# Polynomial attention: state formed straight from scaled keys in 32x32 tiles, values of the four groups in different rows, outputs added up and projected once

## What is computed

```python
qkv = x @ W_attn
q, k, v = jnp.split(qkv, 3, axis=-1)       # 16 heads of 8 columns
...
att = jnp.einsum('bhid,bhjd->bhij', q, k) * (1.0 / math.sqrt(hd))
causal = jnp.tril(jnp.ones((T, T), dtype=bool))
att = jnp.where(causal[None, None], att, -jnp.inf)
att = polymax(att)      # s > 0: (s*s + 1)/1000; -100 <= s <= 0: (1 - 0.01*s)/1000; else 0
y = jnp.einsum('bhij,bhjd->bhid', att, v)
...
return y @ W_proj
```

## Time and profile before

| | |
|---|---|
| time, median of 3 runs | 3188.33 us (3187.82 to 3189.63) |
| the profiled execution's own time | 3197.16 us |
| its span, first to last instruction | 3195.4 us |
| mean granted TensorE clock | 0.919 of full |
| attention stage touched here | about 667 to 1341 us of the span |
| length of its steps | about 34 us; about 44 for the third group of an element in the loop; 48 with `finish` |

### The profile page before, as it was taken

The page is one execution under the profiler, slowest core; times in us unless marked ns, Lnnn a source line. Parts: engine busy times, 40 slices in busy tenths (PEclk is TensorE's granted clock), DMA queues, the critical chain, the costliest instruction groups (busy, mean ns, idle before and its releaser), DMA issues. The chain is left out here.

```text
span 3195.4 us, 55424 instructions
## 1 busy us (share of the span) xinstructions
PE 2832.2 (89%) x15400; PEld 1924.1 (60%) x15400; DVE 2087.3 (65%) x5242; ACT 1199.9 (38%) x2164; POOL 836.7 (26%) x1220
## 2 busy tenths in 40 slices
PE   5999999958787888689999998869989989999986
PEld 4777777735555555467777776445465465465453
DVE  6777777747676777577777776355556556555533
ACT  2111111127565657521111111335545545545532
POOL 1222332225555555423222332001101101111100
PEclk8999999958888788899999998879999999999988
DMA  3000000000000000110000000000000000000000
GB/s 130 0 0 0 0 0 0 1 0 2 3 2 3 2 2 2 61 44 0 0 0 0 0 0 1 0 1 1 1 2 1 1 1 1 1 1 1 1 1 27
DMA packets 12996, 23.60 MB, mean 7 GB/s; under 512 B 2306, under 2 KB 7682, under 8 KB 12804
## 3 DMA queue, kind: packets, MB, share of 16 engines
q1 hardware_dynamic: 12804, 21.22, 2.0%
HBM read 18.52 MB, written 2.10 MB: 6 GB/s over the span
## 5 line engine op out<-in xcount | busy, mean ns | idle before, releaser
L555 DVE SCALAR_TENSOR_TENSOR moe_acc<-moe_ps,moe_comb,moe_acc 128x512 f32<-128x512 f32 x896 | 661.1, 744 | 174.5 <-PE moe_ps L304 167.9
L2017 DVE CUSTOM_DVE_ANT_0 attn_masked<-attn_psm,attn_causal 128x1024 f32<-128x1024 f32 (+7 forms) x512 | 367.6, 755 | 210.4 <-PE attn_psm L1742 199.3
L1921 ACT ACTIVATE attn_probs<-attn_pse 128x512 f32<-128x512 f32 (+1 forms) x640 | 319.9, 553 | 301.6 <-PE attn_pse L1756 301.0
L304 PE MATMUL moe_ps<-moe_Wg,moe_xh 128*128 128x512 f32 x1024 | 329.4, 403 | 25.0 <-DVE moe_Wu L501 25.0
L335 PE MATMUL moe_ps<-moe_Wd,moe_ih 128*128 128x512 f32 x1024 | 337.8, 411 | 0.0
L304 PE MATMUL moe_ps<-moe_Wu,moe_xh 128*128 128x512 f32 x1024 | 337.1, 411 | 0.0
L1772 PE MATMUL attn_psy<-attn_probs,attn_V 128*64 128x512 f32 (+3 forms) x1536 | 325.5, 524 | 0.3 <-POOL attn_probs L1677 0.3
L454 POOL TENSOR_SCALAR moe_part<-consts,moe_pick,moe_prob 128x8 f32<-128x8 f32 x256 | 98.1, 398 | 752.1 <-ACT moe_prob L389 752.1
L1677 POOL TENSOR_SCALAR_AFFINE_SELECT attn_probs<-attn_probs 128x256 f32<-128x256 f32 (+1 forms) x192 | 95.1, 495 | 757.7 <-ACT attn_probs L1921 757.7
L1021 POOL TENSOR_TENSOR attn_R<-attn_R 128x1024 f32<-128x1024 f32 (+1 forms) x128 | 215.5, 1690 | 201.6 <-DVE attn_R L1365 201.4
L1756 PE MATMUL attn_pse<-attn_qS,attn_kS 110*128 110x512 f32 (+3 forms) x768 | 233.2, 394 | 21.4 <-ACT attn_probs L1921 15.2
(11 more groups left out here) (208 smaller groups left out, 4871.2 us busy)
## 6 DMA issues: line engine op xcount, KB each, us to landing
moe_stageg<-in_w_gate SPq DMA_DIRECT2D x8, 512.0 KB, 7.2
moe_stageu<-in_w_up SPq DMA_DIRECT2D x8, 512.0 KB, 8.3
moe_stageg<-in_w_down SPq DMA_DIRECT2D x8, 512.0 KB, 3.7
out<-X SPq DMA_DIRECT2D x1, 2048.0 KB, 8.9
attn_qS<-attn_mh SPq DMA_DIRECT2D x64, 4.0 KB
attn_qS<-attn_ml SPq DMA_DIRECT2D x64, 4.0 KB
attn_wd<-in_wd SPq DMA_DIRECT2D x1, 864.0 KB, 5.7
attn_w<-in_wqkv SPq DMA_DIRECT2D x1, 768.0 KB, 5.1
```

The lines of the kernel that those rows point to most:

```text
L304: last = pe.matmul(expert_bank[j % 4][:, :], a[q][:, :], w[b][:, cols], start=k == 0, stop=k == 2)
L555: dve.scalar_tensor_tensor(acc[:, q, r, :], expert_bank[j % 4][:, :], comb[:, q, r, e:e + 1], acc[:, q, r, :], ALU.mult, ALU.add).then_inc ...
L1921: act.activation(probs[:, u % 2, c, HALF - n:HALF], e_bank[c][:, HALF - n:HALF], ACT.Exp, scale=SCORE_SCALE).then_inc(p_ready, 1)
L2017: dve.tensor_tensor_reduce(masked[:, k % 2, 0:n], m_all[:, base:base + n], causal[:, SEQ - n:SEQ], 1.0, NEG, ALU.add, ALU.max, mx[:, q, v: ...
```

## The change

- **State.** `state` on GpSimd and its buffers and semaphores are gone. `run` is now made from keys that are already scaled: the weights have a fourth block of 128 columns, the key weights times -0.01 (`FACTORS`), and the keys in `KV` come from that block. `run` is double-buffered. `values` takes it as it is: each chunk is 4 matmuls, one per head, on a tile of 32 rows and 32 columns at a place on the array's diagonal, in full float32, in place of one 128x128 fp32r matmul. The wait on `S_ready` becomes one on `av_ready`, ahead of the last unit's values.
- **Values in different rows.** The four groups' values stand at rows 0, 16, 8 and 24 of a head's 32 (`V_FROM`, `V_TO`; for odd groups `KV` is read 16 columns off). The other rows are zero.
- **Outputs.** `yS` holds one sum. Group 0 is copied by ScalarE as before; for groups 1 to 3 VectorE adds `y_bank` to it (`add_out`), once at unit 4, ahead of `highest`, and once at the end of the step, ahead of `correct`. `finish` projects once: 8 matmuls in place of 32.
- ScalarE's copy to `KV` has 16 columns of 32 in place of 24. The weights' rounding at the start is 4 operations on ScalarE and 4 on VectorE in place of 2 and 2. The loaded weights grow by a third, the projection's shrink to a quarter.

```diff
-GW = 3 * P
+GW = 4 * P
...
-        KV = [sb(f"KV{q}", [P, BT, 2 * P]) for q in range(2)]
-        run = sb("run", [P, BT, P])
-        runm = sb("runm", [P, BT, P])
-        runl = sb("runl", [P, BT, P], F32R)
-        S = [sb(f"S{q}", [P, BT, P], F32R) for q in range(2)]
+        KV = [sb(f"KV{q}", [P, BT, 2 * (P + q * WINDOW)]) for q in range(2)]
+        run = [sb(f"run{q}", [P, BT, P]) for q in range(2)]
         R = sb("R", [P, SLOTS, GH, HALF])
         T0 = sb("T0", [P, GH, HALF])
         seen_one = sb("seen_one", [P, P])
-        yS = sb("yS", [P, GROUPS, SEQ])
+        yS = sb("yS", [P, SEQ])
...
+        def parts(q, j):
+
+            half = P + q * WINDOW
+            both = KV[q][:, j:j + 2, :].rearrange("p j (a n) -> p (j a) n", n=half)
+            return both[:, :, 0:P].rearrange("p a (n c) -> p a n c", c=ROW)[:, :, :, 0:WINDOW]
...
-                for s in (runm_ready, runl_ready, S_ready, sq01_ready):
-                    pool.sem_inc(s, LEAD)
-                pool.memset(run[:, 0, :], 0.0).then_inc(zero_ready, 1)
+                pool.sem_inc(sq01_ready, LEAD)
+                for q in range(2):
+                    pool.memset(run[q][:, 0, :], 0.0).then_inc(zero_ready, 1)
                 pool.wait_ge(w_in, 48)
                 pool.tensor_scalar(seen_one[:, :], seen[:, 0:P], 1.0 + LIFT * LIFT, None, ALU.mult).then_inc(seen_set, 1)
                 for q in range(2):
-                    pool.tensor_copy(KV[q][:, :, :], kv_ones.unsqueeze(1).to_broadcast([P, BT, 2 * P])).then_inc(kv_set, 1)
-
-                def state(m, q):
-
-                    pool.wait_ge(av_ready, after(m * NU + NU - 1))
-                    pool.wait_ge(y_ready, after((m - 1) * 2 - 1))
-                    pool.tensor_tensor(runm[:, :, :], run[:, :, :], state_mask.unsqueeze(1).to_broadcast([P, BT, P]),
-                                       ALU.mult).then_inc(runm_ready, 1)
-                    pool.wait_ge(runm_ready, after(m))
-                    pool.sem_inc(pool_pause, 1)
-                    pool.tensor_tensor(runl[:, :, :], runm[:, :, :], k_low.unsqueeze(2).to_broadcast([P, BT, P]),
-                                       ALU.mult).then_inc(runl_ready, 1)
-                    pool.wait_ge(runl_ready, after(m))
-                    pool.tensor_tensor(S[q][:, :, :], runm[:, :, :], f32(runl[:, :, :]), ALU.subtract).then_inc(S_ready, 1)
...
-                    if has_next:
-                        state(m + 1, (g + 1) % 2)
-
-                pipeline(pool, lambda: state(0, 0), step, lambda b, more: None)
+
+                pipeline(pool, lambda: None, step, lambda b, more: None)
...
-                                last = pe.matmul(a_bank[:, h * 2 * P:(h + 1) * 2 * P], xT[a][:, j * P:(j + 1) * P], w[b_][:, g, P:GW],
+                                last = pe.matmul(a_bank[:, h * 2 * P:(h + 1) * 2 * P], xT[a][:, j * P:(j + 1) * P], w[b_][:, g, 2 * P:GW],
...
                     if first:
                         pe.wait_ge(yc_ready, after(m * 2 + s - 1))
+                    if end:
+                        pe.wait_ge(av_ready, after(m * NU + NU - 1))
...
-                        pe.wait_ge(S_ready, after(m))
                         chunks = [c for c in range(4 * s, 4 * s + 4) if c]
                         for c in chunks:
-                            last = pe.matmul(y_bank[:, (c % 4) * P:(c % 4 + 1) * P], S[q][:, c, :], qS[q][:, c * P:(c + 1) * P],
-                                             start=False, stop=c == chunks[-1], skip_group_check=True)
+                            for j in range(GH):
+                                rows = slice(j * ROW, (j + 1) * ROW)
+                                last = pe.matmul(y_bank[rows, (c % 4) * P:(c % 4 + 1) * P], run[q][rows, c, rows],
+                                                 f32(qS[q][rows, c * P:(c + 1) * P]), start=False, stop=c == chunks[-1],
+                                                 skip_group_check=True)
...
-                            for g in range(GROUPS):
-                                c = s * HALF + j * P
-                                last = pe.matmul(e01[1][:, s, j * P:(j + 1) * P], yS[:, g, c:c + P], wp[:, g * DIM:(g + 1) * DIM],
-                                                 start=g == 0, stop=g == GROUPS - 1)
+                            c = s * HALF + j * P
...
-                act.activation(w[0][:, :, 0:P], w32[:, :, 0:P], ACT.Copy, scale=SCORE_SCALE)
-                act.activation(w[0][:, :, P:GW], w32[:, :, P:GW], ACT.Copy).then_inc(w_high, 1)
+                for k, factor in enumerate(FACTORS):
+                    act.activation(w[0][:, :, k * P:(k + 1) * P], w32[:, :, k * P:(k + 1) * P], ACT.Copy,
+                                   scale=factor).then_inc(w_high, 1)
...
-                        act.activation(KV[g % 2][:, 2 * i:2 * i + 2, :].rearrange("p j (g c) -> p (j g) c", c=ROW)[:, :, 0:3 * HD],
-                                       a_bank[:, :].rearrange("p (n c) -> p n c", c=ROW)[:, :, 0:3 * HD],
+                        act.activation(parts(g % 2, 2 * i), a_bank[:, :].rearrange("p (a n c) -> p a n c", a=4, c=ROW)[:, :, :, 0:WINDOW],
...
                 def copy_out(m, g, s):
-                    act.wait_ge(y_ready, after(m * 2 + s))
-                    act.activation(yS[:, g, s * HALF:(s + 1) * HALF], y_bank[:, :], ACT.Copy, scale=1.0 / DIVISOR).then_inc(yc_ready, 1)
+                    if g == 0:
+                        act.wait_ge(y_ready, after(m * 2 + s))
+                        act.activation(yS[:, s * HALF:(s + 1) * HALF], y_bank[:, :], ACT.Copy, scale=1.0 / DIVISOR).then_inc(yc_ready, 1)
...
-                        dve.wait_ge(runm_ready, after(m - 1))
+                        dve.wait_ge(y_ready, after((m - 1) * 2 - 1))
...
-                            ins = dve.tensor_tensor(run[:, c + 1, :], a_bank[:, h * P:(h + 1) * P], run[:, c, :], ALU.add)
+                            ins = dve.tensor_tensor(run[q][:, c + 1, :], a_bank[:, h * P:(h + 1) * P], run[q][:, c, :], ALU.add)
...
                             diagonal(m, g, k + 1)
+                        if k == NQ0 + 1:
+                            add_out(m, g, 0)
...
+                    add_out(m, g, 1)
                     correct(dve, dve_pause, m, g % 2, lambda: low_weights(m, g), ((cc_ready, US), (cm_ready, 2 * ND), (cy_ready, 2)))
+
+                def add_out(m, g, s):
+                    if g:
+                        dve.wait_ge(y_ready, after(m * 2 + s))
+                        y = yS[:, s * HALF:(s + 1) * HALF]
+                        dve.scalar_tensor_tensor(y, y_bank[:, :], 1.0 / DIVISOR, y, ALU.mult, ALU.add).then_inc(yc_ready, 1)
...
+WINDOW = 2 * HD
+V_FROM = (0, 0, HD, HD)
+V_TO = (0, WINDOW, HD, WINDOW + HD)
+FACTORS = (SCORE_SCALE, 1.0, SLOPE, 1.0)
...
+    for g in range(GROUPS):
+        w[:, g, 3, :, V_FROM[g]:V_FROM[g] + HD] = wqkv[2][:, g]
+        wp[:, V_TO[g]:V_TO[g] + HD] = a["L0_attn_W_proj"].reshape(GROUPS, GH, HD, DIM)[g]
```

More of the change, by code:

```diff
@@ L1484, in attn0_laid_out @@
     small[:, 4:8] = np.arange(P)[:, None] // ROW == np.arange(GH)
-    same = (np.arange(P)[:, None] // ROW) == (col[None, :] // ROW)
-    small[:, 8:136] = same * np.where(row < 24, SLOPE, np.where(row < 26, 1.0 - HALF_LIFT * HALF_LIFT, 0.0))[:, None]
-    small[:, 136:264] = ((row == 24) | (row == 25))[None, :]
-    small[:, 392:904] = np.tile(np.triu(np.ones((P, P))), (1, 4))
+    small[row == 24, 8], small[row == 25, 8], small[row == 26, 8] = lift_parts(np)
+    small[:, 9], small[:, 10] = -LIFT, HALF_LIFT
@@ L1489, in attn0_laid_out @@
+    small[:, 12:12 + P] = np.where(row == 24, 1.0 - HALF_LIFT * HALF_LIFT, 0.0)[None, :]
+    small[:, 12 + P:] = np.tile(np.triu(np.ones((P, P))), (1, 4))
     r["attn0_small"] = small
```

50 lines of the change are left out of this document (26 added, 24 removed).

## The result

The changed kernel takes 3222.32 us (median of 4 runs, 3216.13 to 3222.82), beside 3188.07 us for the kernel before (4 runs, 3187.57 to 3189.63). The ratio is 1.0102, with a 95% interval of 1.0085 to 1.012. The forecast was 3191.3 us and the range ended at 3206, so both were wrong by a clear margin: some 31 us are missing from the sum.

A forecast was written before the change was run, and what follows sets the result against it. No engine is full, so waits decide, TensorE's longest for the keys' eviction. Terms 15.0 + 4.4 - 16.6 - 1.8 + 2 = +3.0 us on a median of 3188.33 gave 3191.3 us, range 3179 to 3206.

The forecast's parts named there:

- State matmuls: Middle and end of each step on TensorE: small tiles replacing 128x128 matmuls cost +15.0 us (11.8 to 18.2).
- The changeover: One more switch between tile shapes at each middle and end of a step: 0.1 us each, 3.2 us in all.
- the rival of the tiles one by one: Rival: diagonal tiles do not overlap on TensorE, 86 us in place of 15, giving 3262 us; chance 8%.
- VectorE's jump behind `y`: Step's end: VectorE fetches code only after `y_ready`, +2 us (0 to +12); rival of a late jump, 3203 us, 17%.
- the sign of that rival: Step's end: `take` starting more than 3.5 us behind `y` would show the forecast wrong.
- GpSimd's relief: Step's end: VectorE's pair is faster without GpSimd's passes, -1.8 us (-6 to 0); rival going further, 3179 us, 20%.
- The addition ahead of the peak: Middle of a step: VectorE adds half of `y` before reading the peak, +4.4 us (3 to 6).
- Finish: Shorter projection at four finishes, -16.6 us (-18 to -12); rival that the saving isn't had, 3199 us, 7%.
- The clock was let stand: Attention stage: TensorE's mean clock of 0.84 was assumed unchanged, with no term in the sum.
- the last of the prediction's signs: After jumps: half-clock phases growing or shrinking from the mean clock of 0.84 would show the forecast wrong.

The follow-up runs named there:

- i1: The changed kernel with the small state matmuls put ahead of the constant term's four 128x128 matmuls instead of behind them, in both halves; 3209.43 us, ratio 1.0053.
- f1: The changed kernel with the second half's 16 state matmuls moved from the step's end to behind unit 3; 3188.22 us, ratio 0.999.
- f3: The kernel before with the four state matmuls at the step's end cut into 16 of 128 rows by 32 columns, full float32; 3234.41 us, ratio 1.014.
- h4: The changed kernel with VectorE's mid-step addition placed behind the peak instead of ahead of it; 3222.19 us, ratio 1.0095.
- h5: The changed kernel with the second half's 16 state matmuls behind unit 3 and VectorE's mid-step addition behind the peak; 3177.10 us, ratio 0.9958.
- f6: The kernel before with only the outputs' part of the change; the state stays on GpSimd in 128x128 matmuls; 3190.04 us, ratio 1.0005.
- h7: The changed kernel with state matmuls moved behind units 1 (first half) and 3 (second half), and VectorE's mid-step addition behind the peak; 3178.98 us, ratio 0.9966.
- f2: The changed kernel with the second half's 16 state matmuls moved from the step's end to behind unit 8; 3202.03 us, ratio 1.0038.

## Why the prediction was wrong

Point by point, in its own steps.

**State matmuls: the price near right, and the failed step is right behind it.** The tiles run as priced: the next matmul starts 0.79 us behind the first of 12 (0.76 was the price), and 16 took 1.01 in i1, as priced. The changeover ahead of them was mis-sized: 0.17 us at each of the 32 places (1.09 less 0.91), where 0.1 was taken. From the start of the constant term to the end of `y` it is 0.50 us more in a middle and 0.61 more at an end, 17.8 us in place of 15.0 and near the upper end of 18.2. The tiles on the diagonal do run four at a time, and the rival of the tiles one by one (3262 us) is out. (That rival's "+30 us" for two at a time comes to some 20 more than the term of 15 by its own 0.23 a matmul.)

Then the prediction says that TensorE "has just been busy there, and both places are ahead of what everyone waits for, so nothing hides it". True of their duration; but the step costed the new matmuls by how long they last, and never asked what the old ones had been hiding. There were 8 records of the state ahead of the jump, and now there are 64. The sequencer comes to the jump some tens of records ahead, and 28 of these small ones are worth 0.66 us.

**The jump of TensorE: the missing term, some +34 us.** This is the step that failed. The prediction had the number in hand. It read "2.09 us of jump" in the earlier trace rows and "0.72" in the earlier trace rows, wrote "still within the 2.09 of the jump", and let both stand as constants. They were remainders: 0.7 us to the branch, a branch of 3.4 and 0.5 behind it, less the 3.05 by which the load was ahead. 12 ends by 2.53 and 4 finishes by 2.50 are 40.4 us. Of these the wait of 6.6 us at the next keys' piece is got back, so some 34 are left. Only VectorE's jump was a rival.

**VectorE's jump behind `y`: the wrong engine.** Priced at +2, with 12 more as a rival. Its branch takes 0.06 us. `take` does start 4.9 us behind `y` on average and not 3.5, which I had named as the sign of that rival. Yet the row says that it waits for the scores of TensorE, 0.78 us behind their start. The sign came true by another mechanism.

**GpSimd's relief: the size below what was there.** It was -1.8 in the sum. The pair takes 2.35 us, and `take` stands 0.86 us behind the start of the scores, where it stood 1.58 before. At 12 ends these 0.7 us are 8.7 us that were won back out of the 40. Two things can do this, and either is enough. With the jump closed (f1) it is 0.78, by the short pair alone; in f3, which keeps GpSimd's passes, it is 0.7 to 1.0 at the eight ends with a long branch, by the late scores alone. So the 8.7 us are not the relief's own.

**The addition ahead of the peak: right in the trace, not in the time.** TensorE's next piece comes 0.38 later in step 3, where 0.44 was said, and its wait for the peak rose from 4.4 us in 3 steps to 6.8 in 11. In time neither is shown: h4, without this cost, is no faster by anything that its runs can tell, and h5 is 10 us faster than f1, more than the rows explain.

**Finish: right by itself.** From the start of the projection to the next scores it took 10.82, 11.22 and 8.59 us before, and 6.16, 5.91 and 5.96 after: 4.66, 5.31 and 2.63 less. At the fourth it is 20.51 and 13.58 us to the first matmul of the next stage, 6.93 less. That is 19.5 us for the four, where 16.6 was the price. But the first three start 2.2 to 2.4 us later and the fourth 3.1, so the next scores come 10.0 to 10.6 us behind `y` and not 8.7. And by f6 about half of the saving hangs on GpSimd's relief.

**The clock was let stand: right over the stage.** In the stretch of the earlier trace rows it is 0.81 where it was 0.84, which looks like the last of the prediction's signs. But from 700 to 1320 us it is 0.82 in both, as shown at f1.

**The sum again**, with what was measured: 17.8 for the tiles, 4 for the peak, -19.5 for the four finishes, 40.4 for TensorE's jump, -6.6 at the keys' piece and -8.7 at `take` are +27.4 us. From the first matmul of the stage to that of the next the two traces differ by 27.5 (672.9 and 700.5). That it closes so well is luck in part: at two ends the gains at the keys' piece and at `take` lie beside each other and may count once, and some shorter waits are in no term. The medians differ by 34.2, since the profiled execution of before stood 8.8 above its median and that of after did not. The prediction put those 8.8 us down to the profiler. But 25 more runs of the kernel before went from 3183.59 to 3198.46, so it lies within the spread of its runs.

## What to carry to other kernels

A jump hides behind what is queued ahead of it. In these kernels this cover was 20 to 44 records, whatever work they held: so keep long matmuls last before a branch, and put small ones a few units earlier. A wait marked "issue" behind a branch is the rest of two numbers, the branch and the lead; look up both (the rows of the flag's load and of the branch) before an edit near a jump is costed. And where an edit cuts few long instructions into many short ones, price what stands behind them as well.

## What the runs showed of the hardware that I had not expected

- TensorE's branch takes 2.7 (f3) to 3.9 us (h7) on average, single ones from 0.35 (f3) to 5.05 (f1), and those of VectorE and ScalarE 0.045 to 0.074 us at the same jump. In the four of f1 that took 4.7 to 5.05 us two packets of 16384 bytes stand within the branch, one 0.35 to 0.5 us behind its start and one 1.0 to 1.5; in the usual ones there is one. It may be that a block fetched in sequence goes ahead of the one that is needed; that is not shown.
- The flag is loaded with 28 records of TensorE's work still ahead in four of the kernels, with 36 to 44 in others and with 20 in f2. The Trainium skill, "TensorE: Matmul & The Clock Gate", section Architectural detail: the array is 16× 32×32, not 1× 128×128, gives TensorE's queue a depth of 64; no run here shows that number, the most counted is 44 not started, or 48 not ended.
- Four 32x32 tiles on the diagonal that all write one PSUM bank ran together: 12 full-float32 matmuls of 128 columns in 0.86 us and 16 in 1.08, just as column tiles of 128x32 did (16 in 1.08). Going over to them from 128x128 matmuls cost 0.17 us at each of 32 places. The Trainium skill's "TensorEngine Tiling (Array Packing)", section Restrictions and Gotchas, would not have them access one bank at once; the measurement decides, for tiles in different rows of PSUM. What the prediction cites from the skill's "PSUM — Partial Sum Buffer" is said there of two engines; for row tiles of TensorE that page repeats the Tiling rule.
- A VectorE pair with two SBUF inputs took 4.50 us beside a pass of GpSimd (f6) and 2.35 without one (after). The kernel before had both, 4.51 and 2.37; so this is GpSimd's doing and not the change's.
